# Seven edits to the written-out order of a state-space layer followed by a mixture of experts

## The reference

```python
x = x + layernorm(attn(layernorm(x)))
x = x + layernorm(ffn(layernorm(x)))
# attn, with N = 16 states, R = 64
xc, z = split(x @ W_in.T)
xs = silu(conv3(xc))
x_dbl = xs @ W_x.T                       # 64 columns for dt, 16 for B, 16 for C
dt = softplus(dt_param @ W_dt.T + b_dt) + 1e-5
A = exp(-exp(A_log) * dt);  Bx = B * dt * xs
s = A_t * s + Bx_t                       # scan over time, for 256 x 16 states
y = (C @ W_C.T) * sum_n(s) + D_param * xs
out = (y @ W_out.T) * silu(z)
# ffn, with F = 1024, E = 8, TOP_K = 2
h = gelu(x @ W1[e] + b1[e]);  y_e = h @ W2[e] + b2[e]
out = sum_e(y_e * combine_e) + gelu(x @ sW1 + sb1) @ sW2 + sb2
```

## Time and profile before

| | |
|---|---|
| median of 3 runs | 1249.29 us (1247.64 to 1250.5) |
| profiled execution: time | 1254.36 us |
| its span, first to last instruction | 1252.6 us |
| TensorE's mean granted clock | 0.901 of full speed |
| PE busy | 1047.0 us (84%) |
| DVE busy | 684.6 us (55%) |
| ACT busy | 625.9 us (50%) |
| POOL busy | 704.9 us (56%) |

### The profile page before, as it was taken

One profiled execution on the slowest core, in us unless ns is written; L12 is line 12 of the kernel. 1 busy time (PEld: TensorE's weight loads), 2 busy tenths in 40 slices (PEclk: granted clock), 3 DMA queues, 4 the chain that ended last, 5 costly groups with the idle time before them and its releaser, 6 DMA issues. The chain is left out here.

```text
span 1252.6 us, 15512 instructions
## 1 busy us (share of the span) xinstructions
PE 1047.0 (84%) x4736; PEld 833.6 (67%) x4736; DVE 684.6 (55%) x1216; ACT 625.9 (50%) x1190; POOL 704.9 (56%) x701
## 2 busy tenths in 40 slices
PE   4555588877777886897988898989999999999995
PEld 2122265655555555575877686869999999999884
DVE  1699998998987889974996350101111111111035
ACT  3784869687486685667654431212232222322234
POOL 2496968768479797588675257224343333332233
PEclk9676789898878887897989899889999999999998
DMA  6000010202002006132431595359998888897252
GB/s 181 18 29 5 34 35 18 68 1 84 1 18 68 1 21 225 43 73 59 115 80 58 183 266 152 66 157 349 335 311 269 262 279 252 257 276 221 50 177 101
DMA packets 140931, 162.68 MB, mean 130 GB/s; under 512 B 27976, under 2 KB 125984, under 8 KB 140832
## 3 DMA queue, kind: packets, MB, share of 16 engines
q1 hardware_dynamic: 124976, 142.70, 35.4%
q0 software_dynamic: 15872, 18.99, 7.9%
HBM read 135.20 MB, written 26.87 MB: 129 GB/s over the span
## 5 line engine op out<-in xcount | busy, mean ns | idle before, releaser
L1538 POOL TENSOR_TENSOR Ssum<-Ssum,S 128x512 f32<-128x512 f32 x240 | 301.3, 1270 | 84.7 <-DVE S L1151 84.0
L1013 PE MATMUL psum<-w,hT 128*128 128x256 f32 x1152 | 260.6, 384 | 5.0 <-issue 5.0
L1588 POOL DMA_INDIRECT acc_d<-y,ID x72 | 114.3, 1587 | 244.2 <-DMA acc_d<-y,ID 122.5
L1013 PEld LDWEIGHTS psum<-w,hT 128*128 128x128 f32 x1152 | 219.9, 193 | 34.8 <-issue 4.9
L1420 ACT ACTIVATE A<-dts,nea 128x512 f32<-128x512 f32 x256 | 178.0, 720 | 85.8 <-DVE S L1151 59.3
L1459 ACT ACTIVATE hT<-psum,bb 128x256 f32<-128x256 f32 x200 | 83.3, 470 | 251.3 <-PE psum L980 199.8
L980 PE MATMUL psum<-XT,w 128*128 128x256 f32 x800 | 189.9, 394 | 13.2 <-issue 10.8
L980 PEld LDWEIGHTS psum<-XT,w 128*128 128x128 f32 x800 | 156.9, 198 | 44.9 <-issue 21.8
L1127 DVE TENSOR_TENSOR psum<-us,psum 128x512 f32<-128x512 f32 x256 | 163.5, 683 | 38.6 <-PE psum L901 36.7
L1151 DVE TENSOR_TENSOR_SCAN S<-A,carry,psum 128x512 f32<-128x512 f32 x120 | 148.6, 1265 | 0.0
L1285 DVE TENSOR_TENSOR y<-bb,psum 128x256 f32<-128x256 f32 x72 | 26.9, 416 | 214.0 <-PE psum L1013 199.0
(11 more groups left out here) (150 smaller groups left out, 1318.8 us busy)
## 6 DMA issues: line engine op xcount, KB each, us to landing
w<-W SPq DMA_DIRECT2D x94, 1024.0 KB
bb<-b SPq DMA_DIRECT2D x47, 128.0 KB
xnb<-x SPq DMA_DIRECT2D x16, 256.0 KB, 2.9
Xr<-x SPq DMA_DIRECT2D x16, 256.0 KB
x_d<-gb SPq DMA_DIRECT2D x8, 512.0 KB
xn_d<-nb SPq DMA_DIRECT2D x8, 512.0 KB, 3.6
X<-x_d SPq DMA_DIRECT2D x16, 256.0 KB, 8.4
ACC<-acc_d SPq DMA_DIRECT2D x16, 256.0 KB, 6.0
```

What stands on the lines that cost most here:

```text
L1013: t = eng.matmul(bank(g)[:, 256 * k:256 * k + 256], hT[n % 2][:, f, 128 * k:128 * k + 128], w[:, f, :], start=f == 0, stop=f == 7)
L1538: eng.tensor_tensor(to, to, of, ALU.add).then_inc(nsum, 1)
L1588: eng.indirect_dma_start(acc_d, bass.IndirectOffsetOnAxis(ap=ID[:, col, 1:2].bitcast(u32), axis=0), y[n % NY][:, k, :], None, compute_op=A ...
```

## The change

Seven edits: (1) each scan of an odd chunk waits for its own copy of `carry`; (2) two more empty steps stand between softplus and dt_sum, and prep is spread over steps 0 to 27; (3) one product `dbc` of 128 rows (blocks of 32 rows: 16 of B or, in the last, C, then 16 of dt's) takes the place of `dtc` and `bp`; W_dt is padded with zero rows to 128; ACT copies it once in fp32 and once in bf16; (4) W_x is loaded by 8 DMAs in place of 5, without the memset that they waited for; (5) list entries are issued and waited for in sets: rounds 0 and 1 are a set each, round 2 is cut into sets of 3 groups with four yields between; (6) LATE is 5: the shared groups of chunk 5 are held back too, six in all; (7) 54 calls for a chunk in place of 48.

```diff
-FIRST_POST, LAST_POST, FIRST_PREP, LAST_PREP = 0, 27, 0, 25
-LATE = 6
+FIRST_POST, LAST_POST, FIRST_PREP, LAST_PREP = 0, 27, 0, 27
+LATE = 5
...
+SET = 3
+SETS = [ROUTED[a:b] for a, b in zip([0] + TILES, TILES[:-1])]
+SETS += [ROUTED[a:a + SET] for a in range(TILES[-2], len(ROUTED), SET)]
+SET_OF = {group: n for n, groups in enumerate(SETS) for group in groups}
...
-        d, p, t0, t1 = (next(use) for _ in range(4))
-        say("dtc", i, d)
-        yield
-        say("bp", i, p)
-        say("dtc_out", i, d)
-        yield
-        say("bp_out", i, p)
+        d, t0, t1 = (next(use) for _ in range(3))
+        say("dbc", i, d)
+        yield
+        yield
+        say("dbc_out", i, d)
         yield
...
         say("softplus", i, t0, t1)
         say("low_out", i)
+        yield
+        yield
         yield
         yield
...
-        for m in range(TILES[r - 1] if r else 0, TILES[r]):
-            say("ids", m)
-        if r == NR - 1:
-            for m in range(NHALF):
-                say("ids", NT + m)
-        for _ in range(4):
-            yield
-        listed[0] = TILES[r] if r < NR - 1 else len(ROUTED)
+        for n in range(r, r + 1 if r < NR - 1 else len(SETS)):
+            say("ids", n)
+            for _ in range(4):
+                yield
+            listed[0] += len(SETS[n])
...
-                calls = 48 if listed[0] else 26
+                calls = 54 if listed[0] else 26
...
-        bp32 = xnb[0:96, 0:2, :].rearrange("p j d -> p (j d)")
+        bp32 = xnb[0:64, 0:2, :].rearrange("p j d -> p (j d)")
...
-        def wait_ids(eng, r):
-
-            eng.wait_ge(got_id[r], 16 * (TILES[r] - (TILES[r - 1] if r else 0) + (NHALF if r == NR - 1 else 0)))
+        def wait_ids(eng, group):
+
+            n = SET_OF[group]
+            eng.wait_ge(got_id[n], 16 * sum(len(units(g)) for g in SETS[n]))
...
                     for k in range(2):
-                        t = eng.matmul(ps[0:80, :], wx[:, k, 0:80], xs[i % 2][:, k, :], start=k == 0, stop=k == 1)
-                    t.then_inc(full[BANK[g]], 1)
-                elif step == "bp":
-                    i, g = a
-                    ps = take(g)
-                    for k in range(2):
-                        t = eng.matmul(ps[0:96, :], wx[:, k, 80:176], xs[i % 2][:, k, :], start=k == 0, stop=k == 1)
+                        t = eng.matmul(ps, wx[:, k, :], xs[i % 2][:, k, :], start=k == 0, stop=k == 1)
                     t.then_inc(full[BANK[g]], 1)
...
-                        if k == 0:
-                            eng.wait_ge(carried, CARRIES * (i // 2 + 1))
+                        eng.wait_ge(carried, CARRIES * (i // 2) + (k + 1 if k < 2 else 3 + (k - 2) // 4))
...
-                    eng.copy(dcb[i % 2], ps[0:80, :]).then_inc(dtc_out, 1)
-                elif step == "bp_out":
-                    i, g = a
-                    ps = evacuate(g)
+                    eng.copy(dbc[i % 2], ps).then_inc(dbc_out, 1)
                     if i >= 2:
                         eng.wait_ge(mult, 32 * (i - 1))
-                    eng.copy(bp32, ps[0:96, :]).then_inc(bp_out, 1)
                     eng.copy(bst[i % 2], ps[0:96, :]).then_inc(bp_out, 1)
...
-                    eng.wait_ge(bp_out, 2 * i + 2)
-                    eng.tensor_tensor(bp32[0:64, :], bp32[0:64, :], bst[i % 2][0:64, :], ALU.subtract).then_inc(mid, 1)
+                    eng.wait_ge(bp_out, i + 1)
+                    eng.wait_ge(xT_out, 2 * i + 2)
+                    eng.tensor_tensor(bp32, dbc[i % 2][0:64, :], bst[i % 2][0:64, :], ALU.subtract).then_inc(mid, 1)
...
-            eng.wait_ge(wx_zero, 1)
-            for to, fr, n in [(0, 0, 64), (64, 80, 16)] + [(80 + 32 * g, 64, 16) for g in range(3)]:
-                eng.dma_start(wx[:, :, to:to + n], wxv[:, :, fr:fr + n]).then_inc(got_wx, 16)
-            eng.dma_start(wdc[0:64, :], W_dtT).then_inc(got_v, 16)
-            eng.dma_start(wdc[64:80, :], W_CT).then_inc(got_v, 16)
+
+            for k in range(4):
+                eng.dma_start(wx[:, :, 32 * k:32 * k + 16], wxv[:, :, (80 if k == 3 else 64):][:, :, 0:16]).then_inc(got_wx, 16)
+                eng.dma_start(wx[:, :, 32 * k + 16:32 * k + 32], wxv[:, :, 16 * k:16 * k + 16]).then_inc(got_wx, 16)
+            eng.dma_start(wdt, W_dtT).then_inc(got_v, 16)
+            eng.dma_start(wc, W_CT).then_inc(got_v, 16)
...
```

More of the change, by code:

```diff
@@ L522, in finishing @@
     say("result", NC - 1)
-TAKING = {"xT", "nT", "xc", "z", "dtc", "bp", "dt", "cmat", "wout", "logit", "count", "turn", "up", "down"}
-GIVING = {"xT_out", "nT_out", "xc_out", "z_out", "dtc_out", "bp_out", "dt_sum", "yadd", "gated", "lg_out",
+TAKING = {"xT", "nT", "xc", "z", "dbc", "dt", "cmat", "wout", "logit", "count", "turn", "up", "down"}
+GIVING = {"xT_out", "nT_out", "xc_out", "z_out", "dbc_out", "dt_sum", "yadd", "gated", "lg_out",
           "place", "turn_out", "up_out", "down_out"}
@@ L546, in emptied @@
         return "xc_out", 6 * i + 3 * n + 3
-    if step == "dtc":
-        return "dtc_out", i + 1
-    if step == "bp":
-        return "bp_out", 2 * i + 2
+    if step == "dbc":
+        return "bp_out", i + 1
     if step == "dt":
@@ L672, in build @@
         wxz = put("wxz", [128, 2, 512])
-        wx = put("wx", [128, 2, 176])
-        wdc = put("wdc", [80, 256])
+        wx = put("wx", [128, 2, 128])
+        wdt = put("wdt", [128, 256])
         wout = put("wout", [128, 2, 256])
@@ L725, in build @@
         zs = [put(f"zs{i}", [128, 4, 256]) for i in range(2)]
-        dcb = [put(f"dcb{i}", [80, 512]) for i in range(2)]
+        dbc = [put(f"dbc{i}", [128, 512]) for i in range(2)]
         bst = [put(f"bst{i}", [96, 512], bf16) for i in range(2)]
+        wc = nc.alloc_sbuf_tensor_at("wc", [128, 256], f32, offset=at[0] - 1024).ap()[96:112, :]
         A = [put(f"A{i}", [128, 512]) for i in range(NA)]
@@ L766, in build @@
         xc_out, conv, edged, xs_done, zs_done = (sem(n) for n in ("xc_out", "conv", "edged", "xs_done", "zs_done"))
-        dtc_out, bp_out, mid, mid_out, low, low_out = (
-            sem(n) for n in ("dtc_out", "bp_out", "less_high", "mid_out", "less_mid", "low_out"))
+        dbc_out, bp_out, mid, mid_out, low, low_out = (
+            sem(n) for n in ("dbc_out", "bp_out", "less_high", "mid_out", "less_mid", "low_out"))
         dt_out, softp, dt_done = sem("dt_out"), sem("softplus"), sem("dt_done")
@@ L781, in build @@
         tabled = [sem(f"tabled{i}") for i in range(NR)]
-        got_id = [sem(f"got_id{i}") for i in range(NR)]
+        got_id = [sem(f"got_id{i}") for i in range(len(SETS))]
         got_g = [sem(f"got_g{i}") for i in range(2)]
@@ L867, in _ @@
                     t.then_inc(full[BANK[g]], 1)
-                elif step == "dtc":
+                elif step == "dbc":
                     i, g = a
@@ L1373, in _ @@
                     exp_ln()
-                elif step == "dtc_out":
+                elif step == "dbc_out":
                     i, g = a
@@ L1389, in _ @@
                     eng.wait_ge(mid, i + 1)
-                    eng.copy(bst[i % 2][0:64, :], bp32[0:64, :]).then_inc(mid_out, 1)
+                    eng.copy(bst[i % 2][0:64, :], bp32).then_inc(mid_out, 1)
                 elif step == "low_out":
@@ L1659, in _ @@
                 elif step == "ids":
-                    unit, = a
-                    r = UNIT_ROUND[unit]
-                    eng.wait_ge(select, SELECTED[NR if unit >= NT else r])
-                    if unit in (0, *TILES[:-1]):
+                    n, = a
+                    for unit in (u for group in SETS[n] for u in units(group)):
+                        r = UNIT_ROUND[unit]
+                        eng.wait_ge(select, SELECTED[NR if unit >= NT else r])
                         eng.wait_ge(tabled[r], 32 * len(ROUND[r]))
-                    row = eng.value_load(trow[0:1, unit:unit + 1], min_val=0, max_val=LROWS - (2 if unit < NT else 1))
-                    if unit < NT:
-                        eng.dma_start(ID[:, 2 * unit:2 * unit + 2, :], lists[:, bass.ds(row, 2), :]).then_inc(got_id[r], 16)
-                    else:
-                        eng.dma_start(ID[:, NT + unit, :], lists[:, bass.ds(row, 1), :].squeeze(1)).then_inc(got_id[r], 16)
+                        row = eng.value_load(trow[0:1, unit:unit + 1], min_val=0, max_val=LROWS - (2 if unit < NT else 1))
+                        if unit < NT:
+                            eng.dma_start(ID[:, 2 * unit:2 * unit + 2, :], lists[:, bass.ds(row, 2), :]).then_inc(got_id[n], 16)
+                        else:
+                            eng.dma_start(ID[:, NT + unit, :], lists[:, bass.ds(row, 1), :].squeeze(1)).then_inc(got_id[n], 16)
                 elif step == "fetch":
```

21 lines of the change are left out of this document (11 added, 10 removed).

## The result

| | before | after |
|---|---|---|
| median | 1249.29 us (7 runs, 1245.88 to 1251.37) | 1241.29 us (7 runs, 1237.71 to 1244.12) |
| ratio, 95% interval | | 0.9935 [0.9916, 0.9954] |
| profiled execution, span | 1252.6 us | 1237.3 us |
| last matmul's end to the end | 13.6 us | 10.7 us |

The change gains 8.0 us. The forecast was 17.9 us of gain, 1231.4 us: right in sign and inside its range, but more than twice the gain that was measured.

The account below looks back on a forecast made before the run. DVE bounds the scans up to 692 us, PE the rest. Gains of 0.4 + 5.6 + 1.0 + 1.5 + 1.5 - 2.0 + 7.0 + 2.9 = 17.9 us give a median of 1231.4 us, range 1221 to 1246.

Parts of the forecast that it names:

- edits 6 and 7: Chunks 6 and 7: two more tiles replace shared groups, loading POOL and DVE; 2.0 us of loss.
- start: Program start: more W_x issues cost 1.5 us, the W_dt product starts 2.0 us earlier; 0.4 us gain in the sum.
- carry and softplus (edits 1, 2): DVE's carry and softplus stalls go: 5.6 us in chunk 4, 1.0 in two small stalls, 1.5 in chunk 6.
- one product (edit 3): Fewer matmuls and one ACT copy less count only in chunk 6, where DVE waits for PE: 1.5 us gain.
- sets: At the last list, PE's pause for the first gather goes, with 1.3 us of clock: 7.0 us gain.
- end: Behind the last matmul only chunk 7's statistics are left, chunk 6's being placed earlier: 2.9 us gain.
- The first (SP falls behind): List entries beside weight fetches delay weights and stop PE, 3.5 us for each of seven blocks: 1256 us; chance 0.1.
- The second (1242 to 1244): Chunks 6 and 7 become PE's; denser groups delay spread rows and give back 10 to 13 us; chance 0.2.
- the fourth (1241): Scan stalls only change releaser (POOL's sum, PE); end and list changes stay, 8.3 us gain; chance 0.15.
- The "right" signs: No carry wait, chunk dt_sum waits under 4 us, chunk 5's scan 7 to 9 us after `u`, no G pause, eight blocks.
- "wrong" ones: PE weight pauses at 800 to 870 us, decay waits, spread waits above 45 us, or first scan after 46 us.
- The forecast's estimate: List entries issued behind three 1 MB weight loads land after about 13 us, hidden since sets are listed groups ahead.

Follow-up runs that it names:

- g1: The kernel before itself, run and profiled again: 1249.08 us, ratio 1.0004.
- f1: The kernel before with six shared groups held back in place of four: 1288.0 us, ratio 1.0268.
- e2: The changed kernel with 48 calls for a chunk in place of 54, six groups still held back: 1240.29 us, ratio 0.992.
- g4: The changed kernel again, unaltered, beside other kernels on one chip: 1240.89 us, ratio 0.9938.
- g3: The kernel before with edits 3 to 5 only (old carry wait and old softplus spacing, four groups held back): 1230.89 us, ratio 0.9856.
- g2: The changed kernel without edits 6 and 7, so edits 1 to 5 alone (four held back, 48 calls): 1224.5 us, ratio 0.9804.
- f3: Edits 1 to 5 alone, but with the last list's entries in one block again (edit 5 undone): 1245.57 us, ratio 0.9936.
- i1: The kernel before with two groups held back in place of four: 1248.18 us, ratio 0.9983.
- h2: Edits 1 to 5 alone, plus chunk 6's statistics ahead of the last down and W_x loaded behind the router's weights: 1230.59 us, ratio 0.9826.
- i3: The same kernel as h2, run again: 1218.47 us, ratio 0.9754.
- e1: The changed kernel again, unaltered, in the first set of runs: 1241.4 us, ratio 0.993.
- i4: The same kernel as h1 (e2 with the router's last count earlier), run again: 1234.85 us, ratio 0.9875.
- f2: Edits 1 to 5 alone, four held back, but chunk 5's two shared groups done behind the scans, tiles first: 1236.58 us, ratio 0.986.
- i2: Edits 1 to 5 alone with two groups held back in place of four: 1235.96 us, ratio 0.989.
- the second set: Four kernels run on one chip, among them f1, f2 and f3, beside the kernel before at 1253.82 us.
- the two of the fourth: h1 and h2, the two kernels of the fourth set of runs, beside the kernel before at 1253.17 us.
- h1: e2 with chunk 7's finish taken in faster behind the last scan, to bring the router's last count forward: 1245.13 us, ratio 0.9945.

## Why the prediction was wrong

The step that failed is "edits 6 and 7", put at 2.0 us of loss by the words "So PE's work is moved, not cut". They cost 19.3 us, or 16.4 with the gain at the end. What was moved, and past what, decides. Work that needs no list was moved from before the last list to behind the last tile. With one set PE turns its first listed tile 99.3 us (g1) and 102.2 us (f1) behind the last count, after a wait for the tile's rows. With sets and six groups held back it turns it 59 to 65 us behind the count without a wait, and starts its up matmuls 66.0 us (e2) and 68.1 us (g4) behind it, after a wait for a bias. All that PE has for that time, and for the finish of chunk 7 ahead of it, are the groups that need no list. Each held-back group takes 14.2 us of them away. The earlier trace rows showed the pause which says that this cover was already short, and I read it as a cost of SP alone.

By the terms, forecast against measured:

| term | forecast | measured |
|---|---|---|
| start | +0.4 | about -1.7 (medians of the first scans) |
| carry and softplus (edits 1, 2) | +8.1 | +6.4 (g3 to g2) |
| one product (edit 3) | +1.5 | +3.1 (g1 to g3) |
| sets | +7.0 | +14.6 (g1 to g2), 10.3 with the slow block (f3) |
| six held back and 54 calls, without the end | -2.0 | -19.3 (16.4 of g4 to g2, and the end's 2.9) |
| end | +2.9 | +2.9 |
| sum | 17.9 | 6.0 by these terms, 8.0 by the medians |

Edits 1 to 5 have 17.0 us in the forecast, 22.4 by the measured terms and 24.3 us by the medians (g2). The 1.9 us between these are in no term; the profiled executions differ from their medians by as much.

**Start.** The loss of 1.5 us by three more issues came as forecast: ACT's first instruction stands at 14.62 us in place of 13.11. The gain behind it, 2.0 us, was there in the first profile (first scan 45.62, before 46.03 us) and mostly not in the others. Of the four profiles with the old start three have the first scan at 45.5 to 46.1 us and one at 48.0; of the fourteen with edits 3 and 4, five at 45.6 to 46.5 and nine at 47.7 to 48.4. The two kinds go with the granted clock. Its mean over 27 to 38 us is 0.78 to 0.85 in all eight of these profiles with the early first scan and 0.66 to 0.72 in all ten with the late one; the product with W_x takes 2.5 to 3.4 us in the former and 3.7 in the latter. Like against like the change is small. Before and after in the first pair, both early, differ by 0.4 us, as forecast (though 2.0 less 1.5 is 0.5); i1, the late one of the old start, stands within 0.4 us of the late ones of the new. So the -1.7 of the medians is mostly the late kind coming more often, and whether the edits do that or chance is not shown. h2 and i3 show that the issues were the bound: with W_x behind wg the first scan is at 44.3 us.

**Edits 1 and 2.** The mechanism was right for chunk 4: no carry wait, and POOL's sums as the next bound. The first scan of chunk 5 is 9.0 us earlier in the first pair of profiles. In chunk 6 the softplus stall of 9.42 us is gone. The waits for spread rows stay there (15.8 us, against 17.4 in the earlier trace rows), and the new wait of 6.0 us for a tile's transposed rows has come. From g3 to g2 the first scan of chunk 5 comes 4.9 us closer to the first of all and that of chunk 7 7.3 us, against 5.6 and 8.1 in the forecast.

**Edit 3.** I put nothing outside chunk 6. Between g1 and g3, which both have the old waits, the first scan of chunk 4 comes 3.6 us closer to the first scan of all (276.1 against 279.7 us), and that of chunk 7 3.1 us closer. So it counted in chunks 1 to 3, where I had called it hidden, and not in chunk 6.

**Sets.** The place was right, the size was half. The number was read from one execution in which PE had lost 11 us just before, in a slow stretch that the argument passed over (771 to 788 us). Of those 11 us only 3.8 show at 28 left less 32 left (74.8 against 71.0 us), since the pause for G took up the rest.

**Six held back.** In the changed kernel the 16 us come in two pieces, as g4 against g2 shows: the last count is 12.1 us later, and from 33 to 28 left takes 75.7 us in place of 70.4. Between the last scan and the count PE is idle for 12.1 us in g4 and 6.0 in g2; 8.4 us of it is one wait for `nb` of chunk 7 (both profiles of the changed kernel and e1 have it). On ACT the gelu of two groups and their table loads stand ahead of it. ACT's timeline in the changed kernel:

```profile
707.74 1.28 ACT L1460 ACT_TABLE_LOAD   x1
709.03 3.71 ACT L1460 ACTIVATE hT<-hT 128x2048 f32<-128x2048 f32 x2
712.76 1.28 ACT L1308 ACT_TABLE_LOAD   x1
714.06 1.09 ACT L1329 ACTIVATE nb<-gb,scale 128x256 f32<-128x256 f32 x2
```

With 48 calls (e2) the count is not held up by such a wait but has 4.0 groups of PE's work between it and the last scan in place of 2.2 in g2, and the list costs 14.4 us more. With the count early (i4) the list costs nothing, and the loss is ahead of it. With the same tiles beside the scans but two shared groups behind them (f2) nearly all is back. That it is the two groups of cover is shown by f1, f2, i1 and i2, from both sides; how each order turns the missing cover into pauses ahead of the count or behind it is read from the profiles and not settled by an experiment of its own. The wait for `nb` was not taken away by itself.

**Rivals.** The first (SP falls behind) is refuted: the entries go out in eight sets and PE's waits for weights are small. The second (1242 to 1244) and the fourth (1241) had nearly the right time, mostly for wrong reasons. Of the second, spread rows came later in chunk 7 (14.8 us of waits against 9.0), but not in total (37.6 against 36.7), and g4's last scan ends 1.1 us behind g2's (2.9 with its earlier start), not 10 to 13. Of the fourth, the 6.0 us wait in chunk 6 is a stall with a new releaser, but 6.4 us of edits 1 and 2 are there in g3 to g2. That its 1241 us was met is luck.

**The signs named ahead.** The "right" signs came true: no carry and no softplus wait in the chunks, the first scan 6.75 us behind `u` (7 to 9 were named), no pause for G, eight blocks, one chunk's statistics behind the last matmul. Of the "wrong" ones two showed: a pause of PE for weights at the list, 3.0 us in g4 (1.4 us in the first profile, just behind the stretch named), and a first scan later than 46 us, in g4 and e1 though not in the first profile. None of them looked at the step with the largest error. Its sign would have been the time of the last count and PE's first listed tile.

The condition of the first rival was there, though its cost was not. In g4 the entries of the first two sets landed 1.6 to 2.7 us after their issue, and those of the third, issued at 812.6 to 816.4 us behind weight loads, after 8.0 to 8.5 us. The rows are the DMA issues of that stretch (KB each, median us to landing):

```profile
w<-W SPq DMA_DIRECT2D x2, 1024.0 KB, 8.4
...
ID<-list_d SPq DMA_DIRECT2D x2, 3.0 KB, 8.4
ID<-list_d SPq DMA_DIRECT2D x2, 1.5 KB, 8.1
```

The rule of the Trainium skill ("DMA: Bandwidth & Descriptors", section "Queues, rings and completion order") is that each DMA engine takes its descriptors in ring order. By that rule the traces agree. The forecast's estimate was 13 us, and the distance from a set to its gather hid what there was. Biases behind weights come late in the same way and are not hidden everywhere: in e2 PE waits 5.93 and 3.15 us for them, in i1 6.65 us.

## What to carry to other kernels

When a step is moved behind something, ask what it was covering. A pause in the profile says that its cover is used up. From there independent work taken away costs: two groups, 28 us of work, cost 16 to 19 us here and 34 us in f1. A pause read from one execution is a remainder, not a price: whatever delays the waiting engine earlier makes it smaller, so look for slow stretches ahead of it, or take a second profile. And of a change with several parts, price the smallest-looking one too: here one constant ate two thirds of what the others gained.

## What the runs showed of the hardware

- A block of 32 matmuls took 13 to 23 us in place of 7.07, PE idle for 0.2 to 1.8 us between single matmuls with no releaser shown, in seven profiles (the first of before, the four of the second set and the two of the fourth), and in none of the thirteen others. It is an up block in five and a down block in f1 and f2. In the three sets without it the medians of the kernel before were 1248.8, 1249.05 and 1250.3 us, in the two with it 1253.8 and 1253.2; the first profile of before, at 1254.36 us, stands apart from its own seven runs (1249.29) in the same way. So the forecast was read from a disturbed execution. The stretch begins 26 to 37 us behind the last count, while POOL writes the last list or just behind. Its cause is open. In six of the seven no instruction load runs on the DMA queues during it, which speaks against PE waiting for one. It costs the kernel before 4 us and the kernels with sets 10 to 12 (h1 to i4, h2 to i3).
- The granted clock and PE's pauses go together: in chunk 4 of the changed kernel PE is busy 57.29 of 84.38 us at 0.78, before 64.81 of 89.20 us at 0.81, and g2's stretch behind 33 left, without a pause, has 1.00. No run took one without the other.
- One kind of SP's issues is slow while the DMA engines are full, the 128 KB bias of the second weight. In the kernel before it took 0.44 us in the median of 47, and over 1 us in 15 of them, up to 6.16 us. In the changed kernel the last entry of one set and the first of the next stand 8.4 us apart for this reason. The timeline of SP:

```profile
816.74 0.39 SPq L1663 DMA_DIRECT2D ID<-list_d  x1
817.96 0.38 SPq L1684 DMA_DIRECT2D w<-W  x1
818.53 5.81 SPq L1685 DMA_DIRECT2D bb<-b  x1
825.16 1.56 SPq L1665 DMA_DIRECT2D ID<-list_d  x2
```
